# Routed experts on their own rows, by indirect DMA, for three of four sequences; the two attentions' steps mixed; extra matmuls between heads

## What is computed

```
x = x + tanh(g_xattn) * xattn(layernorm(x), ctx)          # 128 wide, 512 keys, softmax
X = layernorm(x)
h = rmsnorm(X);  q, k, v = h@wq, h@wk, h@wv                # 16 heads of 8, 256 keys
X = X + softmax(q k' / sqrt(8)) v @ wo
h2 = rmsnorm(X)
probs = softmax(h2 @ router_w);  topw, topi = top_k(probs, 2);  topw = softmax(topw)
shared = swiglu(h2, sh_gate, sh_up, sh_down)               # 128 -> 256 -> 128
spec = sum over the 8 experts e of combine[t, e] * swiglu(h2, e_gate[e], e_up[e], e_down[e])
x = x + tanh(g_ffn) * (X + shared + spec)
```

## Time and profile before

| what | us |
|---|---|
| median of 3 runs (lowest, highest) | 263.63 (261.04, 266.65) |
| the profiled execution | 264.06 |
| its span in the trace | 262.3 |
| PE busy, DVE busy, ACT busy, POOL busy | 228.3, 156.4, 94.0, 44.2 |

### The profile page before, as it was taken

One profiled execution on the slowest core, in us unless ns is written; L12 is line 12 of the kernel. 1 busy time (PEld: TensorE's weight loads), 2 busy tenths in 40 slices (PEclk: granted clock), 3 DMA queues, 4 the chain that ended last, 5 costly groups with the idle time before them and its releaser, 6 DMA issues.

```text
span 262.3 us, 4103 instructions
## 1 busy us (share of the span) xinstructions
PE 228.3 (87%) x1455; PEld 174.0 (66%) x1455; DVE 156.4 (60%) x410; ACT 94.0 (36%) x206; POOL 44.2 (17%) x73
## 2 busy tenths in 40 slices
PE   7898976577889889897989978689999989999994
PEld 5566865456655456565646555377888868989884
DVE  2879988948443435443453763324788786564553
ACT  2254633232354434432353426524233242122220
POOL 5666430700000000170014200140011000000000
PEclk9999999959785555555555569979999999999999
DMA  6900040220000000021000200000000000000002
GB/s 181 238 0 5 0 120 2 56 66 0 0 2 1 2 0 0 2 76 44 0 2 1 62 0 0 0 2 0 4 0 0 2 0 0 2 0 2 2 0 80
DMA packets 3732, 6.28 MB, mean 24 GB/s; under 512 B 416, under 2 KB 1696, under 8 KB 3712
## 3 DMA queue, kind: packets, MB, share of 16 engines
q1 hardware_dynamic: 3712, 6.02, 8.0%
HBM read 5.50 MB, written 0.52 MB: 23 GB/s over the span
## 4 chain that ended last, share of the span: by engine, by line
PE 63%; DVE 22%; ACT 7%; issue 5%; DMA 1%; POOL 1%; SPq 0%; DVEq 0%; ACTq 0%; POOLq 0%
PE bank L1040 12%; PE bank L1026 7%; PE bank L987 6%; PE bank L1057 5%; PE bank L1059 5%; PE bank L1058 5%; PE bank L1004 5%; DVE mxs L766 5%; PE bank L1010 4%; PE bank L921 3%; ACT ep L516 2%; PE bank L940 2%; DVE silu L787 2%; DVE small L634 1%; DVE vx L794 1%
## 5 line engine op out<-in xcount | busy, mean ns | idle before, releaser
L766 DVE TENSOR_REDUCE mxs<-bank 128x2 f32<-128x512 f32 x64 | 41.2, 686 | 31.1 <-PE bank L987 31.0
L516 ACT ACTIVATE ep<-bank 128x512 f32<-128x512 f32 x64 | 34.7, 595 | 57.1 <-PE bank L1010 57.1
L1040 PEld LDWEIGHTS bank<-down_s,vx 128*128 128x128 f32 x288 | 36.1, 199 | 1.7 <-issue 0.4
L1040 PE MATMUL bank<-down_s,vx 128*128 128x128 f32 x288 | 36.5, 282 | 0.0
L987 PE MATMUL bank<-k,q 32*128 32x256 f32 x128 | 22.4, 439 | 11.4 <-DVE mxs L766 11.3
L1057 PE MATMUL bank<-h2hi,whi 128*128 128x512 f32 x72 | 31.1, 432 | 1.2 <-DVE vx L797 0.9
L987 PEld LDWEIGHTS bank<-k,q 32*128 32x128 f32 x128 | 14.2, 267 | 23.8 <-DVE mxs L766 12.2
L1058 PE MATMUL bank<-h2lo,whi 128*128 128x512 f32 x72 | 28.9, 401 | 0.0
L1059 PE MATMUL bank<-h2hi,wlo 128*128 128x512 f32 x72 | 28.8, 400 | 0.0
L1026 PE MATMUL bank<-ep,vh 128*32 128x256 f32 x256 | 26.0, 545 | 0.0
L778 DVE SCALAR_TENSOR_TENSOR x<-bank,cw,x 128x128 f32<-128x128 f32 x64 | 18.0, 344 | 12.7 <-PE bank L1040 12.5
(11 more groups left out here) (141 smaller groups left out, 323.2 us busy)
## 6 DMA issues: line engine op xcount, KB each, us to landing
raw<-expert_w SPq DMA_DIRECT2D x9, 256.0 KB, 2.7
down_s<-expert_w SPq DMA_DIRECT2D x9, 128.0 KB, 2.7
ctxT<-ctx_T SPq DMA_DIRECT2D x1, 672.0 KB, 8.6
xs<-x_tiles SPq DMA_DIRECT2D x2, 256.0 KB, 4.6
out_dram<-x SPq DMA_DIRECT2D x2, 256.0 KB, 2.0
ffn_s<-ffn_w SPq DMA_DIRECT2D x1, 261.0 KB, 8.6
attn_s<-attn_w SPq DMA_DIRECT2D x1, 242.0 KB, 2.8
ctxT<-ctx_T SPq DMA_DIRECT2D x1, 224.0 KB, 5.2
```

The costliest lines, as they stand in the source:

```text
L516: nc.scalar.activation(ep[:, n % NEP].rearrange("p t s -> p (t s)"), b_of(("exp", n))[:], ACT.Exp, scale=SCALE_H).then_inc(free(("exp", n) ...
L766: nc.vector.tensor_reduce(mxs[:, half % 2, :, c:c + 1], b_of(("max", n))[:].rearrange("p (t s) -> p t s", t=TB), AX_X, ALU.max).then_inc(f ...
L1040: last = pe.matmul(b_of(("down", n))[:, j * D:(j + 1) * D], act_t[:, n % 2, f, j * P:(j + 1) * P], down_s[:, e, f * D:(f + 1) * D], start= ...
```

## The change

Five things change.

1. **Routed experts of sequences 0 to 2 on their own rows alone.** The 6 row tiles of three sequences (`TS`) are routed together at slot 76. A step "rank" at slot 77 counts with small matmuls (L1164 to L1168) how many rows before each row go to the same expert, and DVE turns this into a row number for each of the two choices of each row (`pos`) and an expert for each of 19 tiles of 128 places (`offsets`; `NSLOT` = 19 is enough for any routing). POOL puts the rows of h2 in their places in DRAM with 12 indirect DMAs (L502), SP loads them back in five DMAs (`rows_in`), and each tile is turned (L1264), multiplied with the weights of its expert, which PE finds by reading `offsets` into a register (L1274 and L1295), turned again (L1287), and multiplied down. The results go to DRAM (L369), 12 indirect DMAs on POOL bring them back (L510), and DVE adds them (`combine`).
2. **The dense items are of one sequence (256 rows)**: the shared expert of each sequence, and all 8 routed experts of sequence 3 alone. Shared items 0 to 2 come at slots 46, 62 and 77, both parts at once; the 19 tiles from slot 86 on; the other 9 items last.
3. **The x steps are a list written by hand**, of which 27 steps come one by one between "a" slots 0 to 26; the k stacks of sequences 1 to 3 are emptied by ACT, no longer by DVE.
4. **One extra matmul of 128 x 512**, whose result nobody reads, ahead of the scores of each pair of heads in slots 28 to 62 (L1182; 18 of them).
5. `ep` has 6 buffers instead of 8; `vx`, `probs`, `silu` and others share one tile `early`; the selector's tile later holds h2's high and low parts.

The pieces of the diff are, in their order: the tables, the sizes, POOL's scatter (behind its norm of sequence 2), PE's extra matmul, PE's two steps with a register read, and DVE's `combine`, the last step of the list.

```
+NSP = 3
+MIXED_STEPS = ["f3", "s4", "h1", "g3", "k1", "p4", "s5", "e1", "o4", "xn3", "p5", "q3", "o5", "s6", "n2", "p6", "h2", "s7",
+               "o6", "k2", "p7", "e2", "o7", "n3", "h3", "k3", "e3"]
+SHARED_AT = {0: 46, 1: 62, 2: 77}
+SPARSE_AT = 86
+SPARSE_PER_SLOT = 5
+WARM_SLOTS = range(28, 64)
...
+    NSLOT = (TS * P * 2 + NE * (P - 1)) // P
+    dense = [(0, b) for b in range(NB)] + [(e, b) for b in range(NSP, NB) for e in range(1, NEXP)]
...
+            for t in range(TS):
+                for k in range(2):
+                    nc.gpsimd.indirect_dma_start(slots_row, bass.IndirectOffsetOnAxis(ap=pos[:, k, t:t + 1], axis=0),
+                                                 h2[:, t, :], None).then_inc(rows_put, 16)
...
+                    if slot in WARM_SLOTS:
+                        pe.matmul(b_of(("max", slot))[:], split[:, 0, 0, 0, 0:P], split[:, 0, 0].rearrange("p q s -> p (q s)"),
+                                  start=True, stop=True)
...
+            def gate_up(i):
+                at = pe.value_load(offsets[0:1, 0, i:i + 1], min_val=2 * FF, max_val=NE * 2 * FF)
+                hi = rowsT[:, i // 4 % 2, 0, (i % 4) * P:(i % 4 + 1) * P]
+                lo = rowsT[:, i // 4 % 2, 1, (i % 4) * P:(i % 4 + 1) * P]
+                pe.matmul(bank[:], hi, whi[:, bass.ds(at, 2 * FF)], start=True, stop=False)
+                pe.matmul(bank[:], hi, wlo[:, bass.ds(at, 2 * FF)], start=False, stop=False)
+                pe.matmul(bank[:], lo, whi[:, bass.ds(at, 2 * FF)], start=False, stop=True).then_inc(full(("gu", i)), 1)
+            def rows_down(i):
+                at = pe.value_load(offsets[0:1, 1, i:i + 1], min_val=D, max_val=NE * D)
+                for f in range(2):
+                    last = pe.matmul(b_of(use)[:, (i % 4) * D:(i % 4 + 1) * D], act_r[:, i % 2, f, :],
+                                     down_s[:, f, bass.ds(at, D)], start=(f == 0), stop=(f == 1))
...
+            def combine():
+                for k in range(2):
+                    for t in range(TS):
+                        if k == 0 and t == 0:
+                            dve.wait_ge(rows_back, 16 * 2 * TS)
+                        last = nc.vector.scalar_tensor_tensor(out=x1[:, t, :], in0=back[:, k * TS + t, :],
+                                                              scalar=rs[:, 10 + k, t:t + 1], in1=x1[:, t, :],
+                                                              op0=ALU.mult, op1=ALU.add)
```

More of the change, by code:

```diff
@@ L78, in flamingo_block @@
     NHEADS = NB * NH
-    HALF = NB * L // 2
-    SLOTS_X = NT - TB + SEL_AT + 1
-    def sequence_at(slot, first):
-        b, rest = divmod(slot - first, TB)
-        return b if rest == 0 and 0 <= b < NB else None
+    TS = NSP * TB
+    NSLOT = (TS * P * 2 + NE * (P - 1)) // P
+    NCOUNT = TS
+    groups = [range(NSP), range(NSP, NB)]
+    group_of = [0 if b < NSP else 1 for b in range(NB)]
+    slots_row = nc.dram_tensor("slots_row", [NSLOT * P, D], F32, kind="Internal").ap()
+    slots_out = nc.dram_tensor("slots_out", [NSLOT * P, D], F32, kind="Internal").ap()
     fill_at, read_at = {}, {}
     for b in range(NB):
-        for step, fill, read in M_STEPS + C_STEPS + (ROUTE_STEPS if b % 2 else []):
+        ends = b == groups[group_of[b]][-1]
+        steps = M_STEPS + C_STEPS + (ROUTE_STEPS if ends else []) + (RANK_STEPS if ends and b < NSP else [])
+        for step, fill, read in steps:
             fill_at.setdefault(16 * b + fill, []).append((step, b))
@@ new lines, in flamingo_block @@
+    order = [(name.rstrip("0123456789"), int(name.lstrip("abcdefghijklmnopqrstuvwxyz"))) for name in FIRST_STEPS]
+    mixed = [(name.rstrip("0123456789"), int(name.lstrip("abcdefghijklmnopqrstuvwxyz"))) for name in MIXED_STEPS]
+    left = list(sparse)
+    tanh_items = []
+    for i in range(SLOTS_A):
+        order.append(("a", i))
+        if mixed and i % MIX_EVERY == 0:
+            order.append(mixed.pop(0))
+        for n in range(NSP):
+            if SHARED_AT[n] == i:
+                order += [("up", n), ("down", n)]
+                if i <= last_exp:
+                    tanh_items.append(n)
+        if i >= SPARSE_AT:
+            order += left[:SPARSE_PER_SLOT]
+            left = left[SPARSE_PER_SLOT:]
@@ new lines, in flamingo_block @@
+    order += left
+    for n in range(NSP, ND):
+        order.append(("up", n))
+        if n > NSP:
+            order.append(("down", n - 1))
+    order += [("down", ND - 1), ("end", 0)]
+    pair_uses = {"turn": [], "proj": [("fold", 0)], "sum": [], "misc": []}
+    for stage, i in order:
+        if stage == "xn":
+            pair_uses["turn"].append(("xnT", i))
+        if stage == "q":
+            pair_uses["proj"] += [("q", i), ("v", i)]
+        if stage == "s":
+            pair_uses["sum"].append(("s", i))
+        if stage == "p":
+            pair_uses["turn"].append(("pT", i))
+        if stage == "o":
+            pair_uses["misc"].append(("o", i))
+        if stage == "h":
+            pair_uses["turn"].append(("hT", i))
+        if stage == "k":
+            pair_uses["proj"] += [("qk2", i), ("v2", i)]
+        if stage == "e":
+            pair_uses["proj"] += [(name, i, part) for name in ("stq", "stk") for part in range(2)]
@@ L806, in _ @@
                 elif stage == "a":
                     a_slot(i)
-                else:
-                    m_third(*thirds[i])
+                elif stage == "up":
+                    dense_up(i)
+                elif stage == "down":
+                    dense_down(i)
+                elif stage == "turn":
+                    rows_low(i)
+                elif stage == "gu":
+                    gate_up(i)
+                elif stage == "end":
+                    combine()
         @block.tensor
@@ new lines, in make_stacks @@
+            def make_stacks(b):
+                if b == 0:
+                    pe.wait_ge(sel_ready, 4)
+                pe.wait_ge(hi_ready, b + 1)
+                written(("qk2", b))
+                for qk, name in ((0, "stq"), (1, "stk")):
+                    for part in range(2):
+                        use = (name, b, part)
+                        may_fill(pe, use)
+                        for g in range(2):
+                            for hl in range(2):
+                                last = pe.matmul(b_of(use)[:, g * L:(g + 1) * L], sel[:, qk, hl, 2 * part + g, :],
+                                                 split[:, b % 2, hl, qk, :], start=(hl == 0), stop=(hl == 1))
+                        last.then_inc(full(use), 1)
```

948 lines of the change are left out of this document (558 added, 390 removed).

## The result

| | before | changed kernel |
|---|---|---|
| median, us (lowest, highest; 4 runs each) | 262.66 (261.04, 266.65) | 309.35 (309.08, 314.44) |
| ratio, 95% interval | | 1.180 (1.170, 1.190) |
| its profiled execution, span | 264.06, 262.3 | 309.16, 307.3 |

The changed kernel is 18 per cent slower. The prediction was 252 us with a range of 233 to 273: wrong in sign, and far outside.

A forecast was written before the change was run, and what follows sets the result against it. It saw DVE bound up to slot 0, PE at half clock in slots 28 to 64, PE at full clock from slot 74. Stage terms added up to a 251 us span, 252.8 with 1.8 outside, forecast 252, range 233 to 273.

The forecast's parts named there:

- To slot 0: Start to slot 0: DVE work moved behind it is worth 10.5 us, 4 given back; slot 0 at 34.5 us.
- Slots 0 to 28: Heads with mixed x steps: DVE work 33 us plus 9 idle, so 42 us; ends 36 and 50.
- Slots 28 to 64: Heads with extra matmuls: four fifths of slots at full clock, 64.5 us; ends 59 (full clock) and 87 (half).
- the clock stays at 1.2 GHz: Rival for slots 28 to 64: one extra matmul cannot hold the clock, 87 for 64.5, kernel 274 us; chance 0.16.
- Slots 64 to 74: Last 5 exponential pairs at 2.0 us each and 2 for the turns: 12 us, slot 74 at 153.
- Routing: Routing chain, now exposed behind slot 74: 26 DVE steps, ACT's two and the router's and rank's matmuls, 9.5 us.
- Scatter, load, turn: 12 indirect DMAs at 1.1 us, landing, load and turn before the tiles: 20 us; ends 12 and 39.
- The tiles: 19 tiles at 1.75 us each, plus slow start, drain and waits for ACT and DVE: 39 us; ends 32 and 63.
- The rival that had a read at 0.8: Register reads of 0.8 us each hold up PE's queue: tiles 57 us and not 33, kernel 276; chance 0.12.
- Dense items: 9 last items at 2.4 us plus 2.5 for the last round trip: 24 us, store and gathers (17 us) hidden beside them.
- The end: After the dense items: DVE's 12 additions of 0.29 us and the output's 2.0, 5.5 us.
- The break-even argument of the tiles: 39 us of tiles replace 24 items (55 us of PE), gain 16; scatter's idle and routing take back nearly all.

The follow-up runs named there:

- e14: Changed kernel with the x steps in the order of before and all of them ahead of slot 0: 306.92 us.
- e6: Changed kernel with all 27 mixed x steps ahead of slot 0, in the same hand-written order: 330.91 us.
- e1: Changed kernel with its 27 mixed x steps back in the order of before, 6 groups ahead of slots, the others ahead of slot 0: 287.81 us, ratio to before 1.098.
- e12: Changed kernel with the x steps in the order of before, a second time, on the third chip: 300.49 us.
- e13: Changed kernel unedited, a third time, as yardstick on the third chip: 310.67 us.
- e10: Changed kernel with x steps in the order of before, no extra matmuls and all experts dense for all rows: 272.11 us, ratio to before 1.033.
- e2: Changed kernel without its 18 extra matmuls: 296.70 us, ratio to before 1.136.
- e11: Changed kernel without its 18 extra matmuls, a second time, on the third chip: 300.56 us.
- b1: Kernel before with one extra matmul of 128 x 512 per pair of heads in slots 28 to 62: 264.87 us, ratio 1.006.
- b2: Kernel before with two extra matmuls of 128 x 512 per pair of heads in slots 28 to 62: 262.97 us, ratio 0.992.
- e8: Changed kernel unedited, once more, on the second chip: 305.05 us.
- e7: Changed kernel without the 38 register reads, each tile taking a constant expert's weights: 301.10 us.
- e3: Changed kernel with all 8 routed experts dense for all rows, no rank step, scatter, tiles or gather: 287.47 us, ratio to before 1.100.

## Why the prediction was wrong, step by step

1. *To slot 0*, 34.5: right (34.7), though the terms as they stand add up to 34.1 (40.6 less 10.5 and plus 4).
2. *Slots 0 to 28*, "I take 9 us idle, so 42 us ... 50 is the price": this is the step that failed, 69.7. Two errors. I moved DVE's share only, though the matmuls of 27 steps moved too, and in part ran at a lower clock: 20 us more PE busy. And I let the chains fill idle time for nothing, "the mixed steps fill about half of the rest". Instead this list, as I read it, has about one chain under way at a time, and the pairs of heads wait in it (slots 24 to 26 above). e14 against e6 shows the order alone to be worth 22.6 us, and in place it is worth 16.6 (e1) and 18.5 (e12 against e13); e10, with the same order, has slot 28 at 92.6, 12 us ahead of the changed kernel. No rival had it: the upper end of 50 came from the same reading.
3. *Slots 28 to 64*, 64.5: 70.3, and in other executions 64.2 and 74.3, so the term was right within what it can be known, and that is luck in part. The two ends, 59 and 87, fit: 64.2 at a clock of 0.92, 70.3 at 0.78, 74.3 at 0.71. The reason given for standing near the full end did not hold: the clock is near 0.7 there without extras as well (e2, e11; whether the shared items that are now in the stage do this was not tried), and in b1 and b2 a clock higher by half shortened the stage by 3 us only. The rival "the clock stays at 1.2 GHz" was wrong as well.
4. *Slots 64 to 74*, 12: right (12.0; 10.4 in e2 and e8). *Routing*, 9.5: 13.7; the rank matmuls (L1164 to L1168) took 3.2 us, from 193.7 to 196.9, in a stage whose mean clock is 0.52, and the round trips between them and DVE were not in the sum.
5. *Scatter, load, turn*, 20: 22.4. L502 came every 1.26 us (1.1 said), the load took 3.2 us in the chain (2.7). The group, busy time and mean:

```profile
L502 POOL DMA_INDIRECT slots_row<-h,pos x12 | 11.8, 982 | 16.8 <-DVE pos L867 13.4 <-issue 3.3
```

The last scatter left POOL at 214.6 and landed 2.2 us later, so they overlap; of the two ways to price them that the prediction gives, the one that the Trainium skill ("DMA: Bandwidth & Descriptors", Anatomy of one DMA) leads to if they follow one another, 26 us, is not what happened.

6. *The tiles*, 39: 45.9. The work of a tile was right (1.42; e7 1.37). The register reads were mis-sized: 0.17 each said, 0.26 measured by the length of the phase (e7), which is 3.2 of the 6.9 us. The other 3.7 are there without reads too (36.2 us for the 32.5 that the sum has without them), in the tiles that wait for ACT and DVE, for which 3 was too little. The rival that had a read at 0.8 was much further off; its 57 us for the tiles was not reached, and that the queue runs ahead and hides a part, which stood against it, is what happened. The Trainium skill (the same page, Latency and other measured facts) has a floor of some 600 ns for such a load; this trace has 0.30 us for a TENSOR_LOAD in the median, below that floor.
7. *Dense items*, 24 with the gathers "hidden": 31.9 with the standstill, 22.2 without it (e1). The sum was right and the cover false: in the first profile and on two of the three chips of the experiments the gathers stop DVE and ACT.
8. *The end*, 5.5: 6.7.

The break-even argument of the tiles held in its direction: 24 items of 2.3 us are 55 us and 19 tiles 46, 9 us gained for the 16 said. What takes it back was larger than said. The prediction's own terms, 12 us idle and 9.5 of routing, are already 21.5, more than the 16 of which they were to take "nearly all"; measured, the stretches are 22.4 and 13.7, and e3 gives the balance, 12 us lost without the standstill and 22 with it.

Two of its signs of being wrong came up, the tiles' phase over 45 us (45.9) and slots 28 to 64 over 70 (70.3), but neither points at the stage that lost most; for slots 0 to 28 it named none.

## What to carry to other kernels

A stage belongs to all its engines: when work is moved under another stage, redo the sum for each engine at the clock that holds there, not for the one that bounded it where it was. In an order that each engine follows strictly, a dependent chain holds up all that stands behind it, unless steps of other sequences stand between its links: the same steps in two orders ended at 59.7 and at 82.3 us. Interleave sequences first, and mix with other stages second. Sparse rows pay only if the gain of the products exceeds the scatter and gather that stand exposed: here 9 us were gained on the products and 12 lost in all, 22 with the standstill (e3).

## What the hardware showed unexpectedly

- With 12 indirect gathers of 128 rows under way, ACT and DVE stood still with full inputs, in the first profile for 6.8 and 5.2 us (ACT) and 7.3 us (DVE), between the fourth and the fifth of nine items. It was there in eight of eight such profiles on two chips, and in neither of two on another chip, and each time it ended 3.2 to 3.5 us after the last gather's issue. Plain DMAs of the same size did not do it (one profile), nor did the scatters at 200 to 214 us, beside which DVE worked on, though it had work up to 206.8 only. What the two engines wait for is open; the profile calls it remote, and it was not tried further.
- A register read by PE is a TENSOR_LOAD (0.30 us, the longest 0.72) and some register arithmetic (0.15). With two to a tile, 0.23 to 0.38 us of each stood on the path where nothing else interfered, 0.26 on average (e7): PE's queue hides a part of it only.
- Indirect DMAs of 128 rows leave POOL 1.25 to 1.26 us apart, scatter or gather.
- The clock of one unchanged program varied from 0.71 to 0.92 in slots 28 to 64, and that stage from 74 to 64 us.
- DVE's normalisation of 128 x 128 (L755) took 0.98 us while POOL split weights (L437, L438; 90.14), and 0.30 while POOL was idle (31.57); the mean is 0.63. No run takes the splits away, so that POOL is the cause is not shown.
